# A causal attention and expert kernel on one core: the row maximum of two heads as one VectorE reduction, the mask added by a bf16 matmul

## What is computed

```python
Q = heads(Wq, bq); K = heads(Wk, bk); V = heads(Wv, bv)      # 16 heads of 16
scores = jnp.einsum('bhid,bhjd->bhij', Q, K) / scale
QJ = jnp.einsum('bhid,hde->bhie', jnp.tanh(Q), J_attn)
delta = jnp.einsum('bhie,bhje->bhij', QJ, jnp.tanh(K))
scores = scores + lambda_attn * delta
causal = jnp.triu(jnp.ones((S, S), dtype=bool), k=1)
scores = jnp.where(causal, -jnp.inf, scores)
probs = jax.nn.softmax(scores, axis=-1)
out = jnp.einsum('bhij,bhjd->bhid', probs, V)
```

## Time and profile before

| | us |
|---|---|
| median of 3 runs | 2475.45 |
| lowest, highest | 2470.91, 2476.41 |
| the profiled execution | 2476.85 |
| its span in the profile | 2475.1 |
| TensorE (PE) busy | 2222.3 |
| VectorE (DVE) busy | 1266.8 |
| ScalarE (ACT) busy | 1029.4 |
| GpSimd (POOL) busy | 622.7 |

### The profile page before, as it was taken

The page is one execution under the profiler, slowest core; times in us unless marked ns, Lnnn a source line. Parts: engine busy times, 40 slices in busy tenths (PEclk is TensorE's granted clock), DMA queues, the critical chain, the costliest instruction groups (busy, mean ns, idle before and its releaser), DMA issues. The chain is left out here.

```text
span 2475.1 us, 49744 instructions
## 1 busy us (share of the span) xinstructions
PE 2222.3 (90%) x14878; PEld 1413.3 (57%) x14879; DVE 1266.8 (51%) x3832; ACT 1029.4 (42%) x1752; POOL 622.7 (25%) x1000
## 2 busy tenths in 40 slices
PE   3899989999899999999998298879999999997885
PEld 1345445454445454554454187657777777776674
DVE  4555545555455554555451665434444444443775
ACT  1344444444453444444442132245555555553321
POOL 0012111111111111111121088656100000001786
PEclk9798999999998999999986599989999999999997
DMA  6211222122221222122200554343211111112785
GB/s 208 71 39 42 71 66 80 36 69 71 66 63 42 71 65 80 41 63 71 56 25 26 197 172 162 133 146 130 78 55 55 55 55 54 54 53 100 241 261 186
DMA packets 149366, 223.41 MB, mean 90 GB/s; under 512 B 18512, under 2 KB 104528, under 8 KB 149200
## 3 DMA queue, kind: packets, MB, share of 16 engines
q1 hardware_dynamic: 130000, 173.72, 22.8%
q0 software_dynamic: 15744, 46.16, 5.7%
q10 hardware_dynamic: 3456, 1.34, 0.2%
HBM read 110.26 MB, written 77.33 MB: 76 GB/s over the span
## 5 line engine op out<-in xcount | busy, mean ns | idle before, releaser
L599 DVE CUSTOM_DVE_ANT_0 ps_rows<-ps_rows,maskrow 128x512 f32<-128x512 f32 (+3 forms) x1024 | 480.9, 516 | 430.6 <-PE ps_rows L445 428.0
L546 ACT ACTIVATE probs<-ps_cols 128x1024 f32<-128x1024 f32 (+3 forms) x512 | 360.2, 704 | 531.4 <-PE ps_cols L463 523.2
L445 PE MATMUL ps_rows<-ks,qs 32*128 32x512 f32 (+3 forms) x2048 | 432.1, 507 | 30.8 <-issue 20.9
L459 PE MATMUL ps_cols<-qs,ks 32*128 32x512 f32 (+3 forms) x2048 | 440.0, 507 | 16.0 <-ACT probs L546 16.0
L700 POOL TENSOR_TENSOR pace<-eps 1x1 f32<-1x1 f32 x256 | 46.8, 183 | 1091.1 <-ACT probs L546 1091.1
L463 PE MATMUL ps_cols<-mT,ones_r 32*128 32x512 f32 (+3 forms) x1024 | 298.8, 577 | 0.0
L445 PEld LDWEIGHTS ps_rows<-ks,qs 32*128 32x128 f32 x2048 | 161.5, 192 | 192.3 <-issue 150.2
L1607 DVE TENSOR_TENSOR h_lo<-ps_h,h_hi 128x512 fp32r<-128x512 f32 x135 | 93.3, 691 | 254.4 <-ACT h_hi L1579 254.4
L459 PEld LDWEIGHTS ps_cols<-qs,ks 32*128 32x128 f32 x2048 | 160.0, 191 | 68.8 <-ACT probs L546 61.4
L476 PE MATMUL ps_o<-probs,vt 128*32 128x512 f32 (+3 forms) x2048 | 197.3, 458 | 0.0
L1573 ACT ACTIVATE sg_e<-ps_ge 128x512 f32<-128x512 f32 x135 | 80.7, 598 | 266.6 <-PE ps_ge L1499 266.6
(11 more groups left out here) (200 smaller groups left out, 3885.1 us busy)
## 6 DMA issues: line engine op xcount, KB each, us to landing
xs_d<-zrows SPq DMA_DIRECT2D x45, 384.0 KB, 3.2
xr<-xs_d SPq DMA_DIRECT2D x135, 128.0 KB, 2.0
yo_d<-y_e SPq DMA_DIRECT2D x135, 128.0 KB, 1.7
xn<-in_L_attn_x_dram SPq DMA_DIRECT2D x16, 512.0 KB, 4.3
ks<-k_lin SPq DMA_DIRECT2D x64, 128.0 KB, 2.4
ks<-k_tan SPq DMA_DIRECT2D x64, 128.0 KB, 2.3
qs<-q_lin SPq DMA_DIRECT2D x64, 128.0 KB, 2.6
qs<-q_mix SPq DMA_DIRECT2D x64, 128.0 KB, 2.3
```

What stands on the lines that cost most here:

```text
L445: mm = nc.tensor.matmul(ps_rows[s][:, e, 0:(it + 1) * P], qs[at:at + STRIP, d.par, g, it * P:(it + 1) * P], ks[at:at + STRIP, d.par, g, 0: ...
L459: nc.tensor.matmul(ps_cols[:, e, jt * P:S], ks[at:at + STRIP, b.par, g, jt * P:(jt + 1) * P], qs[at:at + STRIP, b.par, g, jt * P:S], start ...
L546: nc.scalar.activation(probs[:, n % 2, 2 * (1 - s):2 * (1 - s) + 2, jt * P:S], ps_cols[:, :, jt * P:S], ACT.Exp).then_inc(exp_done, 1)
L599: a = nc.vector.tensor_tensor_reduce(out=bank, in0=bank, in1=maskrow[:, (TT - 1 - it) * P:S], scale=1.0, scalar=LOWEST, op0=ALU.add, op1=A ...
```

## The change

In the rows, the mask is now added by TensorE: behind the two score matmuls of a pair stand two matmuls that add `ident_bf` transposed times `mask_bf`, both 128x128 in bfloat16, to the diagonal block of each bank. `mask_bf` holds -1e30 above the diagonal. VectorE then takes the maximum of both banks by one tensor_reduce, and `maskrow` is gone.

```diff
-    maskrow = sb("maskrow", [P, TT * P])
+    ident_bf = sb("ident_bf", [P, P], BF16)
+    mask_bf = sb("mask_bf", [P, P], BF16)
...
-            nc.gpsimd.memset(maskrow[:], 0.0).then_inc(s_id0, 1)
+            nc.gpsimd.memset(ident_bf[:], 0.0).then_inc(s_id0, 1)
+            nc.gpsimd.memset(mask_bf[:], 0.0).then_inc(s_id0, 1)
...
+            nc.gpsimd.affine_select(out=mask_bf[:], in_=mask_bf[:], compare_op=ALU.is_ge, fill=MASK, base=0,
                                     pattern=[[-1, P]], channel_multiplier=1).then_inc(s_id, 1)
...
             for e in range(2):
                 at = STRIP * (2 * s + e)
-                mm = nc.tensor.matmul(ps_rows[s][:, e, 0:(it + 1) * P], qs[at:at + STRIP, d.par, g, it * P:(it + 1) * P],
-                                      ks[at:at + STRIP, d.par, g, 0:(it + 1) * P], start=True, stop=True)
+                nc.tensor.matmul(ps_rows[s][:, e, 0:(it + 1) * P], qs[at:at + STRIP, d.par, g, it * P:(it + 1) * P],
+                                 ks[at:at + STRIP, d.par, g, 0:(it + 1) * P], start=True, stop=False)
+            for e in range(2):
+                mm = nc.tensor.matmul(ps_rows[s][:, e, it * P:(it + 1) * P], ident_bf[:], mask_bf[:], start=False, stop=True)
             mm.then_inc(rows_ready, 1)
...
             dve.wait_ge(rows_ready, pair_no(d, g, it, s) + 1)
-            dve.nop(nofuse=True)
-            for e in range(2):
-                h = 2 * s + e
-                bank = ps_rows[s][:, e, 0:(it + 1) * P]
-                a = nc.vector.tensor_tensor_reduce(out=bank, in0=bank, in1=maskrow[:, (TT - 1 - it) * P:S], scale=1.0,
-                                                   scalar=LOWEST, op0=ALU.add, op1=ALU.max, accum_out=mx[:, gb, it, h:h + 1])
-            a.then_inc(max_done, 1)
+            nc.vector.tensor_reduce(mx[:, gb, it, 2 * s:2 * s + 2], ps_rows[s][:, :, 0:(it + 1) * P], AX.X, ALU.max)\
+                .then_inc(max_done, 1)
```

More of the change, by code:

```diff
@@ L43 @@
 MASK = -1e30
-LOWEST = -3e38
 NSLOT = 2 * NT + NE - 1
@@ L250, in _ @@
             nc.gpsimd.memset(ident[:], 0.0).then_inc(s_id0, 1)
-            nc.gpsimd.memset(maskrow[:], 0.0).then_inc(s_id0, 1)
+            nc.gpsimd.memset(ident_bf[:], 0.0).then_inc(s_id0, 1)
+            nc.gpsimd.memset(mask_bf[:], 0.0).then_inc(s_id0, 1)
             nc.gpsimd.memset(ones[:], 1.0).then_inc(s_id0, 1)
-            pool.wait_ge(s_id0, 4)
-            nc.gpsimd.affine_select(out=ident[:], in_=ident[:], compare_op=ALU.not_equal, fill=1.0, base=0,
+            pool.wait_ge(s_id0, 5)
+            for t in (ident, ident_bf):
+                nc.gpsimd.affine_select(out=t[:], in_=t[:], compare_op=ALU.not_equal, fill=1.0, base=0,
+                                        pattern=[[-1, P]], channel_multiplier=1).then_inc(s_id, 1)
+            nc.gpsimd.affine_select(out=mask_bf[:], in_=mask_bf[:], compare_op=ALU.is_ge, fill=MASK, base=0,
                                     pattern=[[-1, P]], channel_multiplier=1).then_inc(s_id, 1)
[L257 to L262, removed]
+            pool.wait_ge(s_id, 3)
             pool.wait_ge(s_jz, 1)
```

## The result

| | before | after the change |
|---|---|---|
| median, us | 2473.18 (4 runs) | 2956.43 (4 runs) |
| lowest, highest | 2467.59, 2476.41 | 2946.70, 2969.24 |
| the profiled execution | 2476.85 | 2948.42 |
| the loop: first column matmul to last row matmul | 85.1 to 1297.2, 1212.1 | 86.9 to 1781.0, 1694.1 |
| of it with TensorE granted half its clock | 103.5 in 12 stretches | 444.4 in 15 stretches |

The ratio is 1.198 (95% interval 1.194 to 1.202). The forecast was 2839 us, 2790 to 2912: right in its sign and its place, short by 117 us. All the loss lies in the loop, +482 us; what follows it took 12 us less.

What follows compares the result with a forecast made beforehand. TensorE, 90% busy, was taken to bound the kernel. Lost overlap, shape changes and masks gave 471 us, half clock +23; less 122 of absorbed waits and 10 of copy waits, 362 on 2476.85: 2839 us, range 2790 to 2912.

Steps and rivals of the forecast that it cites:

- What bounds: Attention loop: TensorE sets the pace, busy 1154.30 of 1208.70 us; what the change takes off VectorE is off the path.
- (a) to (c): Per block: rows running alone 0.64 us, two array shape changes 0.19, mask matmuls 0.12; 0.95 us more in all.
- (d): Loop: waits where columns already start late for ScalarE's exp absorb 122 us of the added cost.
- (e): Once a batch, TensorE's waits at L389 for ScalarE's copies of k and q shrink, about 10 us in 16 batches.
- +23: Loop: in 26 blocks at half clock the rows cost as much again, 23 us.
- rival 3: The clock: masks and shape changes let it fall 10 us more per batch, 80 us in all, 2920 us; chance 7%.
- 1: Overlap of rows and columns survives the masks; only shape changes and masks are paid, 2560 to 2630 us; chance 8%.
- 5: Faster: masks fit into waits, overlap survives, TensorE's 9.6 us of waits for maxima go, 2467 us; chance 2%.
- 2: Columns' waits for the exp don't shrink because the exp starts later too, 2971 us; chance 5%.
- 4: Mask matmuls pace slower, 0.21 us a block and not 0.10, +57 us, 2895 us; chance 8%.

Runs made afterwards that it cites:

- e1: The change without the two mask matmuls, keeping VectorE's one tensor_reduce per pair; 2460 us, ratio 1.000 to before.
- e7: The change with the logits' moving operand padded by zeros from 8 to 128 columns; 2823 us, ratio 1.144 to before.
- e5: The change with the two full-array mask matmuls moved behind the columns; 2499 us, ratio 1.014 to before.
- e9: The kernel before with a pair's columns on the same strips as its rows, no masks; 2790 us, ratio 1.128 to before.
- e3: The change with mask matmuls of 8 columns in place of 128; 2943 us, ratio 1.200 to before.
- e4: The change with each mask matmul on its rows' strip of 32, a quarter of the mask; 2463 us, ratio 1.002 to before.
- e11: The change with the whole mask as four 32-row matmuls per head on the rows' strips, ahead of the columns; 2822 us, ratio 1.142 to before.

## Why the prediction was right in place and short in size

- *What bounds* held: TensorE is busy 1679 of 1694 us, VectorE's gain shows nowhere (e1).
- *(a) to (c)* held: 1.27 and 0.83 us a block (512 and 256 columns) measured for 1.27 and 0.84. The masks' start-to-start is 0.067 us by the records where I took 0.05, with a smaller load ahead of it; mask to columns is 0.215 where the sum had 0.12 + 0.095.
- *(d)* held; *(e)* was too low, 16 us and not 10, and the 9.6 us of waits for maxima shrank by 6. The sum without its +23 for half-clock blocks was 339 at full clock; 312 were measured, or some 330 if the clock is worth only what e7 shows.
- *The step that failed* is the +23 of half clock, and with it the size of rival 3 ("10 us more in each" batch). I took the stretches at half clock as they were and let only their rows double. Measured: H rose by 341 us, 21 a batch, worth 150 to 170 us and not 23. The mistake was to read the clock's dips as a fixed event. The argument against rival 3, that the masks add no idle time, was true (TensorE is busy 23.90 of 23.90 us) and didn't protect the clock. In the trace of before the dips ended in a loop where four strips mostly work side by side, and the change takes just that away; nothing in my sum asked what ended them. The sign named for rival 3, a granted clock well under 0.96 in the loop, is what came: 0.87.
- *The rivals*: 1 and 5 are out (e5, e9 show what the overlap is worth), 2 is out (17.2 us), 4 is small (the masks' start-to-start of 0.067 us, and in e3 40 us for nearly all of their streaming). Rival 3 was the right one, undersized. That the full-clock part came out within 10% is partly luck: 12 us of waits that went (6 more in (e), 6 for maxima) weren't in the sum, and no run splits the 0.25 us a block that I took as two shape changes and a weight load.

By the Trainium skill ("TensorE: Matmul & The Clock Gate", What's actually happening) the clock follows how busy the engine has been. The row of 739.50 to 763.40 shows TensorE busy 23.90 of 23.90 us at half clock. By that page the stretch should have ended early; here the measurement decides, and in these runs the strips in use tell the average length of the stretches, busy time by the records does not (9.98 of 13.70 us in the shorter one of before).

## What to carry to other kernels

Before a matmul goes between others, look whether those run side by side on different strips. One that needs the whole array, or the same strip, ends their overlap, and its place in the order can cost many times its own length (here 0.97 us a block, clock included, for masks of some 0.12): the same masks cost 20% between rows and columns, 1.4% behind the columns, and nothing when they are cut up for the rows' strips and stand behind the columns. And count the clock in: look in the clock records at what starts each dip and at what works when it ends; thin matmuls that are paced by their weight loads can be padded to full width for almost nothing.

## What I had not expected of the hardware

- An array of which two strips of four work at a time stayed at 1.2 GHz for 23 to 33 us on average behind a trigger, one with four strips at work for 5 to 9 us.
- In e4 the mask matmuls stand ahead of the columns in the program, and by the records they start 0.94 us behind them in the block shown, and behind them in 408 of 498 blocks: on different strips matmuls don't start in program order. The Trainium skill ("TensorE: Matmul & The Clock Gate", The mechanism) has matmuls start strictly in order; here they pass one waiting matmul per strip (e4) and not four (e11). How many may wait between one and four wasn't tried.
- Eight fp32 matmuls (16 records) of 128 columns take 1.98 us where those of 8 columns take 1.88.
